# Which experts of the last layer wait in the weight ring when the graph layer ends: 2 and 3, or 0 and 1

## What is computed

```python
def _L1_ffn_ref(x, Wg, bg, W1, b1, W2, b2):        # x: 1354 x 256, after layernorm
    probs = softmax(x @ Wg + bg)
    _, top_idx = top_k(probs, 2)
    mask = any(top_idx == expert)
    comb = probs * mask
    for e in range(8):
        h = gelu(x @ W1[e] + b1[e])                # W1[e]: 256 x 1024
        y = h @ W2[e] + b2[e]                      # W2[e]: 1024 x 256
        out = out + comb[:, e:e + 1] * y
    return x + out
```

## Time and profile before

| | us |
|---|---|
| three runs | 870.43, 865.66, 869.93; median 869.93 |
| the profiled execution | 866.8, of which 865.0 from the first to the last instruction (the span) |
| PE busy in the span | 769.6 (89%) |
| DVE, ACT, POOL busy | 600.7 (69%), 413.7 (48%), 336.9 (39%) |
| mean granted PE clock | 0.947 of full |

### The profile page before, as it was taken

The page is one execution under the profiler, slowest core; times in us unless marked ns, Lnnn a source line. Parts: engine busy times, 40 slices in busy tenths (PEclk is TensorE's granted clock), DMA queues, the critical chain, the costliest instruction groups (busy, mean ns, idle before and its releaser), DMA issues. The chain is left out here.

```text
span 865.0 us, 13730 instructions
## 1 busy us (share of the span) xinstructions
PE 769.6 (89%) x4212; PEld 581.9 (67%) x4213; DVE 600.7 (69%) x1169; ACT 413.7 (48%) x851; POOL 336.9 (39%) x333
## 2 busy tenths in 40 slices
PE   5999989999999989945999993899858999999994
PEld 4997645555545443434999982687846888888883
DVE  6675857766676779784989875687766666666562
ACT  3336435555655556641666642641353544444441
POOL 2600368677877788044424005000011443333422
PEclk9999979999999999975999996999968999999998
DMA  7538877988898876123345303961482388752110
GB/s 273 212 106 324 201 234 257 281 284 282 289 285 272 268 258 209 35 76 128 137 150 221 124 14 99 452 215 55 166 311 84 76 257 239 237 156 38 31 19 0
DMA packets 61655, 159.02 MB, mean 184 GB/s; under 512 B 20907, under 2 KB 39521, under 8 KB 58403
## 3 DMA queue, kind: packets, MB, share of 16 engines
q1 hardware_dynamic: 40659, 97.97, 33.4%
q0 software_dynamic: 20944, 60.38, 22.3%
HBM read 103.00 MB, written 49.93 MB: 177 GB/s over the span
## 5 line engine op out<-in xcount | busy, mean ns | idle before, releaser
L1892 DVE TENSOR_REDUCE mx<-ps 128x1 f32<-128x452 f32 x264 | 147.7, 623 | 66.0 <-PE ps L1337 65.2
L979 ACT ACTIVATE expo<-ps 128x452 f32<-128x452 f32 x264 | 124.7, 553 | 97.6 <-PE ps L1349 96.6
L1357 PE MATMUL ps<-expo,v_st 128*64 128x452 f32 (+1 forms) x576 | 117.5, 530 | 0.0
L1181 ACT ACTIVATE h<-ps,b_l 128x128 f32<-128x128 f32 x224 | 61.1, 384 | 111.8 <-PE ps L1699 108.9
L1337 PE MATMUL ps<-k_st,q_st 96*128 96x452 f32 x264 | 108.0, 420 | 5.5 <-DVE mx L1892 5.2
L1349 PE MATMUL ps<-q_st,k_st 98*128 98x452 f32 x264 | 97.0, 391 | 4.8 <-DMA q_st<-m_rows 2.6
L913 POOL DMA_INDIRECT out<-y1t,out_row x29 | 46.1, 1591 | 117.8 <-DVE share L2284 94.2
L1337 PEld LDWEIGHTS ps<-k_st,q_st 96*128 96x128 f32 x264 | 50.3, 191 | 53.2 <-DVE mx L1892 36.0
L1716 PE MATMUL ps<-w_ring,h_hi 128*128 x232 | 82.5, 394 | 1.3 <-DVE h_lo L2296 0.5
L843 POOL TENSOR_TENSOR part_lo<-part,part_hi 128x512 fp32r<-128x512 f32 x64 | 82.6, 1316 | 0.5
L896 POOL DMA_INDIRECT x1t<-x_d,goal x29 | 30.0, 1036 | 127.0 <-DVE goal L2251 105.4
(11 more groups left out here) (350 smaller groups left out, 1786.7 us busy)
## 6 DMA issues: line engine op xcount, KB each, us to landing
w_l<-w_l SPq DMA_DIRECT2D x8, 2053.0 KB, 8.2
part<-w_l POOLq DMA_DIRECT2D x32, 512.0 KB, 6.3
w_split_d<-part_hi POOLq DMA_DIRECT2D x32, 512.0 KB, 5.0
w_split_d<-part_lo POOLq DMA_DIRECT2D x32, 512.0 KB, 3.4
adj<-adj_t SPq DMA_DIRECT2D x22, 704.0 KB, 4.3
w_ring<-w_split_d SPq DMA_DIRECT2D x10, 1365.5 KB, 6.8
w_ring<-w_split_d SPq DMA_DIRECT2D x5, 1365.0 KB, 6.3
w_ring<-w_split_d SPq DMA_DIRECT2D x1, 4096.0 KB, 13.5
```

Of the source, the lines that this page charges most:

```text
L979: act.activation(expo[g % 8][:, :], ps[:, 3 + g % 3, 0:QC], ACT.Exp, scale=SCALE).then_inc(s_exp, 1)
L1181: last = act.activation(h1[:, f, :], ps[:, 4 + f // 4, (f % 4) * P:(f % 4 + 1) * P], ACT.Gelu_apprx_tanh, bias=b1_l1[:, bass.ds(e, 1), f])
L1357: return pe.matmul(ps[at:at + 2 * DK, 6 + g // T % 2, lo:hi], v_st[h % 2][:, kt, :], expo[g % 8][:, lo:hi], start=kt < 2, stop=kt == T - 1 ...
L1892: dve.tensor_reduce(mx4[:, n // KB, n % KB:n % KB + 1], ps[:, i % 3, 0:KC], AX_X, ALU.max).then_inc(s_mx, 1)
```

## The change

Experts 0 and 1 now go into slots 2 and 3 beside the graph layer, so expert e lives in slot (e + 2) mod 4. Behind the graph layer SP issues expert 2 in three pieces into slot 0, and nothing of the weights between the row store and the first output store. Behind that store it fetches expert 3 piece by piece into slot 1, and then experts 4 to 7 as before. PE waits with `s_w1` for the one early transfer only; experts 2 to 7 all count on `s_ring`, and `tile_need` asks for them tile by tile. The slot formula takes two more DVE instructions.

```diff
-FIRST_EXPERTS = 16 * (2 + PIECES)
+EARLY = RING // 2
...
-            sp.dma_start(w_ring.bitcast(F32)[:, RING // 2:RING, :], w_split_d[:, RING // 2:RING, :]).then_inc(s_w1, 16)
+            sp.dma_start(w_ring.bitcast(F32)[:, RING // 2:RING, :], w_split_d[:, 0:EARLY, :]).then_inc(s_w1, 16)
...
             sp.wait_ge(s_z, T)
-            sp.dma_start(w_ring.bitcast(F32)[:, 0, :], w_split_d[:, 0, :]).then_inc(s_w1, 16)
-
-            def second_expert(c):
+
+            def ring_piece(e, c):
                 cols = slice(c * SLOTCOLS // PIECES, (c + 1) * SLOTCOLS // PIECES)
-                sp.dma_start(w_ring.bitcast(F32)[:, 1, cols], w_split_d[:, 1, cols]).then_inc(s_w1, 16)
-
-            second_expert(0)
+                sp.dma_start(w_ring.bitcast(F32)[:, (e + EARLY) % RING, cols], w_split_d[:, e, cols]).then_inc(s_ring, 16)
+
+            for c in range(PIECES):
+                ring_piece(EARLY, c)
...
-            for c in range(1, PIECES):
-                second_expert(c)
...
             sp.wait_ge(s_te, 1)
-            sp.wait_ge(s_w1, FIRST_EXPERTS)
-            for e in range(RING, E):
-                due = sp.value_load(ends_due[0:1, e - RING:e - RING + 1], min_val=PRIMED + 1, max_val=PRIMED + TILES1)
-                sp.wait_ge(s_y1_ps, due)
+            for e in range(EARLY + 1, E):
+                if e >= RING:
+                    due = sp.value_load(ends_due[0:1, e - RING:e - RING + 1], min_val=PRIMED + 1, max_val=PRIMED + TILES1)
+                    sp.wait_ge(s_y1_ps, due)
                 for c in range(PIECES):
-                    cols = slice(c * SLOTCOLS // PIECES, (c + 1) * SLOTCOLS // PIECES)
-                    sp.dma_start(w_ring.bitcast(F32)[:, e - RING, cols], w_split_d[:, e, cols]).then_inc(s_ring, 16)
-                    sp.wait_ge(s_ring, PRIMED + 16 * ((e - RING) * PIECES + c + 1))
+                    ring_piece(e, c)
+                    sp.wait_ge(s_ring, PRIMED + 16 * ((e - EARLY) * PIECES + c + 1))
...
-            pe.wait_ge(s_w1, FIRST_EXPERTS)
+            pe.wait_ge(s_w1, 16)
...
-            step(dve.tensor_scalar(beyond, texp[:, :], RING - 0.5, -float(RING), ALU.is_ge, ALU.mult))
-            dve.tensor_tensor(tile_slot[:, :], texp[:, :], beyond, ALU.add)
+            twice = which[:, :, 2]
+            dve.tensor_scalar(beyond, texp[:, :], RING - EARLY - 0.5, -float(RING), ALU.is_ge, ALU.mult)
+            step(dve.tensor_scalar(twice, texp[:, :], 2 * RING - EARLY - 0.5, -float(RING), ALU.is_ge, ALU.mult))
+            step(dve.tensor_tensor(beyond, beyond, twice, ALU.add))
+            dve.scalar_tensor_tensor(out=tile_slot[:, :], in0=texp[:, :], scalar=float(EARLY), in1=beyond, op0=ALU.add, op1=ALU.add)
             loads = which[:, :, 1]
-            step(dve.tensor_scalar(loads, texp[:, :], 1.0 - RING, 0.0, ALU.add, ALU.max))
+            step(dve.tensor_scalar(loads, texp[:, :], 1.0 - EARLY, 0.0, ALU.add, ALU.max))
```

More of the change, by code:

```diff
@@ L1675, in ring_place @@
                 return (pe.value_load(tile_slot[0:1, bass.ds(t, 1)], min_val=0, max_val=RING - 1),
-                        pe.value_load(tile_need[0:1, bass.ds(t, 1)], min_val=PRIMED, max_val=PRIMED + 16 * PIECES * (E - RING)))
+                        pe.value_load(tile_need[0:1, bass.ds(t, 1)], min_val=PRIMED, max_val=PRIMED + 16 * PIECES * (E - EARLY)))
             def up1(t, copied, at_ring=None, bank=2):
```

## The result

| | before | after |
|---|---|---|
| median of 20 runs each, same chip | 868.42 us (863.18 to 877.65) | 862.52 us (858.97 to 872.07) |
| ratio of after to before, 95% interval | | 0.9947 (0.9925 to 0.9968) |
| profiled execution, span | 866.8, 865.0 us | 858.97, 857.2 us |
| mean granted TensorE clock of that execution | 0.947 | 0.954 |

The kernel became faster. The ratio says by 0.53%, 4.6 us, with an interval from 2.8 to 6.5; the medians differ by 5.9. All three readings have the same sign.

The account below looks back on a forecast made before the run. PE was taken as the bound, its savable time being idle time before the last layer's expert loop. An earlier first turn (4.0) plus a held clock (1.85) gave 5.8 us off 868.2, so 862.4 us, range 859.9 to 868.5.

Parts of the forecast that it names:

- Small tables: Ahead of PE's register loads: two added small instructions set `s_te` up to 0.4 us later, at 642.6.
- First turn 4.0 us earlier: Start of the last layer's expert loop: PE turns the first rows at 644.25 instead of 648.24.
- a loss of a third of a microsecond: First gather beside weights: if queues alternate by packet, it loses about 0.34 us; the change gains some 1.7 us.
- Clock held: First turn and first `up1`: PE's clock stays up through two short pauses, 1.85 us more gained; chance 0.50.
- the clock falls all the same: Rival at the first turn and `up1`: no clock gain, only 4.0 us gained, 864.2 us; chance 0.36.
- Output store: First output store in SP's queue moves forward with DVE's additions; nothing of the first five tiles needs it.
- Expert 3 hidden: Expert 3, fetched from about 649, takes 19 us, there by 668 to 670, before tile 7; cost 0.
- Graph-layer load: Beside the graph layer, the same 8 MB move in one transfer with the other two experts' bytes; cost 0.
- a gather that stays slow: Rival: something other than the pieces slows the first gather, landing at 646.8; gain 1.4, 866.8 us; chance 0.08.
- a late loader: Rival: expert 3's pieces delay experts 4 to 7; 878 us at 16.6 us per piece; chance 0.03.

Follow-up runs that it names:

- e1: Changed kernel with the first two pieces of expert 3 issued right behind the row store, PE not waiting for them; 866.81 us, ratio 0.9949 to before.
- e2: Changed kernel with PE also waiting for all of expert 2 ahead of its first register load; 863.58 us, ratio 0.9953 to before.
- e6: Kernel before with 10 unused products on PE ahead of its wait for weights and 2 behind the first turn; 866.84 us, ratio 0.9978.
- e8: Changed kernel itself, run and profiled a second time; 865.85 us, ratio 0.9947 to before.
- e10: Changed kernel itself, run and profiled a third time; 865.16 us, ratio 0.9930 to before.
- e5: Changed kernel with expert 3's pieces held back until three tiles are through the second layer; 877.51 us, ratio 1.0088 to before.
- e3: Kernel before with 19 unused products on PE ahead of its wait for weights and 4 behind the first turn; 868.93 us, ratio 1.0006.
- e4: Changed kernel with 4 unused products on PE ahead of the first turn and 4 behind it; 863.81 us, ratio 0.9946 to before.
- e7: Changed kernel with 2 unused products on PE ahead of the first turn and 2 behind it; 862.92 us, ratio 0.9922 to before.
- e9: Second run of e7, the changed kernel with 2 and 2 unused products on PE; 862.42 us, ratio 0.9921 to before.

## Why the prediction was right, and where it was not

The forecast of 862.4 us stands beside a median of 862.52, and 865.85 and 865.16 in the two repeats (against a before that stood at 868.42, 868.93 and 868.89). That it lies within 0.1 us is luck: before came out at 868.42, near the 868.2 that the forecast started from, but the ratio gives a gain of 4.6 and not 5.8, and one step of the reasoning took what the profiles show as the rarer of two outcomes for the likelier.

1. *Small tables, 0.4 us forecast.* Over-sized. From the first instruction of the block to the one that sets `s_te` are 639.94 - 639.03 = 0.91 us in after and 642.04 - 641.31 = 0.73 before: 0.2.
2. *First turn 4.0 us earlier.* Right, in size and by its reasons: 8.08 - 3.98 = 4.1 after the goals. e1 and e2 show that the transfers, not the wait as such, are what it hangs on: the gather took 5.66 us beside the pieces and 2.81 without. What the prediction set against this, a loss of a third of a microsecond, is refuted: the gather loses 2.85. What fails there is the estimate, which took a turn of the weights' queue to move no more than the gather does; the rule behind it is not refuted. The Trainium skill, "DMA: Bandwidth & Descriptors", section "Queues, rings and completion order", says that an engine takes a whole packet of many descriptors from one queue before it goes on to the next. The trace agrees with that if a piece's share of an engine goes as one packet: a piece of 1365 KB needs 3.3 us at the 422 GB/s measured from 642.0 to 644.9, and the gathers got in when the last one ended. That a share is one packet no run here shows. Only the end was closer than written: the register loads, over at 641.7, and the gather, landed at 641.59, now tie.
3. *Clock held, 1.85 us.* This is the step that failed as a statement of what is likely. The size is right (1.5 in e6, 1.6 between after and e8), and it happened in the profiled execution of after. But with the same instructions the clock fell in e8 and e10, and also in e2, which has one wait more, and in e5, which starts the loop in the same way (first `down1` at 20.63): held once in five profiles. The rival "the clock falls all the same", put at 0.36 with a gain of 4.0, describes the commoner case: 24.87 - 20.56 = 4.3 and 24.87 - 20.58 = 4.3 by the first `down1`. The likeliest gain was thus some 4.3 and not 5.8, and nearer to it lies the ratio too: 4.6 us, 2.8 to 6.5. The rows on which I took the clock as held did not carry that: the pause at 600, where it held, was 1.80 us, and the one ahead of 318, where it fell, 2.21 (PE's timeline of before, the pause in brackets).

```profile
318.74 0.27 PE L1332 MATMUL ps<-const,m_hl 128*22 128x128 f32 x1 [2.21 <-DVE m_hl L1903]
...
601.46 4.84 PE L1622 MATMUL ps<-u_or_h,wgt_keep 128*128 128x258 f32 x21 [1.80 <-DVE nat L2175]
```

The two pauses of the changed kernel, 1.18 and 1.28 us in the execution that held, are 2.46 together, more than either and not between the two.
4. *Output store, nothing.* Right, with a side effect. The fifth gather, issued at 647.6 beside the store and the first piece of expert 3, took 9.3 us; it landed at 656.8, its tile was turned at 660.7, and nothing waited.
5. *Expert 3 hidden, there by 668 to 670.* Right in its effect. The first piece took 11.0 us beside the store, the next two 5.7 and 6.2 (issued at 657.7 and 663.4), so 22.9 us in all and not 19. It was there at 669.6; since all of this profile runs 2.3 us ahead of before, that is 2 us later than forecast, but still 11 us before SP sent the first piece of expert 4 at 680.6 and 18.7 before tile 7 first used expert 3 at 688.3. No PE wait in the loop ends with weights. e5 shows that the cover is real and finite: without it the kernel is slower than before.
6. *Graph-layer load, nothing.* Right as far as the profiles show: the 8 MB took 26.7 us before and 26.6 after, and the row store was issued at 630.3, earlier than the 632.5 of before by what the whole profile was earlier.

The rival of a gather that stays slow is refuted by 2.86 us, and that of a late loader by the landing at 669.6.

What stays open: what makes the clock hold in one execution and fall in another whose windows are nearly the same up to there (0.82 and 0.79 us of PE in the two us up to the first turn). PE's pause ahead of the first turn does not sort them: it was 1.18 us in after, which held, and 1.21 in e10 and 0.80 in e8, which fell. Nor does the time at which the clock had come back to 1.00 after the graph layer: 6.5 us ahead of the goals' end in after, 6.7 in e10, 0.2 in e8. The runs show only that with products in PE's pauses it stayed up in all five profiles, e3, e4, e6, e7 and e9; in e7 and e9 it had come back as late as in e8, 0.2 us ahead of the goals' end.

## What to carry to other kernels

When a wait for a large transfer is moved out of a critical place, look at what else the transfer did there: here the small gather beside it could not start until it was through, and moving the transfer alone was worth five times as much as removing the wait alone (4.2 against 0.8 us). Count a clock that holds "just" as a chance and not as a gain, and profile the same program more than once before you name the cause of 1 or 2 us. A few idle products in a known pause of TensorE are a cheap way to measure what the clock costs there, and may be worth keeping.

## What the hardware showed that was not expected

- A gather of 135 KB takes 2.8 to 2.9 us alone, 5.66 to 5.77 beside 2.7 MB of weights, and 9.3 beside the output store and a piece of weights. Beside the 2.7 MB none of its packets moved until the weights were through (first packet 3.9 us after the issue, 1.7 alone).
- In the changed kernel PE paused 0.8 to 1.2 us before the first turn and 1.3 us behind it, with 0.4 us of work between, and the granted clock fell to half in two of three profiles, 0.9 to 1.3 us after the first `up1` had begun.
- A wait of 3.2 us on PE for weights, in the middle of a loop that was full till then, was followed by ten microseconds at a mean clock of 0.72 (e5).
